# A five-engine instruction order set anew in a two-layer gated cross-attention kernel

## The reference

```python
# layer 0: cross-attention with rotary positions, then a ternary-weight MLP with squared ReLU and a low-rank term
q = rope(layernorm(x) @ Wq.T); k, v = split(ctx @ Wkv.T); k = rope(k)
x = x + tanh(g_xattn[0]) * (softmax(q k^T / 8) v) @ Wout.T
h = bitlinear(layernorm(x), w_fc) + gate * (layernorm(x) @ v.T @ fast_b.T @ u.T)
x = x + tanh(g_ffn[0]) * bitlinear(relu(h) ** 2, w_proj)
# layer 1: a linear mix with a row of the context, then an int8-activation, ternary-weight MLP
x = x + tanh(g_xattn[1]) * (layernorm(x) @ W1.T + mean_row(ctx) @ W2.T + b)
h = gelu(bitlinear(quant(rmsnorm(layernorm(x))), w1) + b1)
x = x + tanh(g_ffn[1]) * (bitlinear(quant(rmsnorm(h)), w2) + b2)
```

## Time and profile before

| | |
|---|---|
| three runs | 1253.99, 1259.77, 1259.27 us; median 1259.27 us |
| the profiled execution | 1254.16 us, of which its span 1252.1 us |
| busy, share of the span | PE 89%, DVE 78%, ACT 63%, POOL 46% |
| mean granted TensorE clock | 0.96 |
| chain of work that ended last | PE 30%, DVE 27%, ACT 20%, DMA 11%, issue 6%, POOL 4% |
| traffic | 140.28 MB, 112 GB/s mean; DMA share 0.91 in the first 135 us, 0.46 from 280 to 1144 us |

### The profile page before, as it was taken

One profiled execution on the slowest core, in us unless ns is written; L12 is line 12 of the kernel. 1 busy time (PEld: TensorE's weight loads), 2 busy tenths in 40 slices (PEclk: granted clock), 3 DMA queues, 4 the chain that ended last, 5 costly groups with the idle time before them and its releaser, 6 DMA issues.

```text
span 1252.1 us, 19955 instructions
## 1 busy us (share of the span) xinstructions
PE 1120.1 (89%) x7102; PEld 697.7 (56%) x7390; DVE 975.9 (78%) x2029; ACT 783.7 (63%) x1509; POOL 577.6 (46%) x564
## 2 busy tenths in 40 slices
PE   5737788989999999999899999999999999999973
PEld 3525546565665656474656565575657465565631
DVE  5998877678779787978877888878876867877672
ACT  2588765758393947576485858385767657585622
POOL 3121465445564644554545455555545443644330
PEclk9757799999999999999999999999999999999997
DMA  9959843463625354444536362637354353524122
GB/s 312 348 141 319 224 117 73 71 130 64 128 54 135 65 113 86 102 98 100 118 64 143 62 142 51 125 66 127 73 95 108 66 115 61 108 58 81 30 59 51
DMA packets 302242, 140.28 MB, mean 112 GB/s; under 512 B 258097, under 2 KB 276017, under 8 KB 300465
## 3 DMA queue, kind: packets, MB, share of 16 engines
q1 hardware_dynamic: 299840, 136.62, 48.7%
q10 hardware_dynamic: 2304, 2.40, 0.6%
HBM read 57.97 MB, written 9.18 MB: 54 GB/s over the span
## 4 chain that ended last, share of the span: by engine, by line
PE 30%; DVE 27%; ACT 20%; DMA 11%; issue 6%; POOL 4%; SPq 2%; POOLq 0%; ACTq 0%; DVEq 0%
PE ps L1734 8%; ACT e L937 5%; PE ps L1782 4%; PE ps L1685 4%; PE ps L1718 3%; ACT rl L975 3%; PE ps L1770 3%; DVE st L1334 3%; DMA pt<-qT 3%; PE ps L1750 3%; ACT hid L980 2%; DVE qT L1347 2%; ACT sq L986 2%; DVE amax L1041 2%; DMA hT<-q 2%
## 5 line engine op out<-in xcount | busy, mean ns | idle before, releaser
L1718 PE MATMUL ps<-xT,fcT 128*128 128x256 f16 x2048 | 261.4, 276 | 7.1 <-ACT rl L975 7.1
L719 POOL TENSOR_TENSOR rs<-ve,nhalf 128x1 f32<-128x1 f32 x160 | 105.3, 660 | 321.7 <-DVE ve L1339 226.4
L1734 PE MATMUL ps<-pjT,hid 128*128 128x512 fp8e4 x1024 | 232.6, 380 | 2.6 <-issue 1.3
L1718 PEld LDWEIGHTS ps<-xT,fcT 128*128 128x128 fp8e4 x2048 | 202.2, 99 | 42.2 <-ACT rl L975 10.2
L744 POOL TENSOR_TENSOR hid<-sq,hid 128x512 f16<-128x512 f32 x128 | 155.9, 1221 | 114.0 <-ACT sq L986 113.6
L1734 PEld LDWEIGHTS ps<-pjT,hid 128*128 128x128 f16 x1024 | 97.7, 98 | 98.9 <-issue 1.3
L1782 PE MATMUL ps<-w2T,hT 128*128 128x512 fp8e4 x512 | 119.9, 389 | 23.0 <-DMA hT<-q 22.8
L975 ACT ACTIVATE rl<-ps,rsf 128x256 f32<-128x256 f32 x256 | 106.5, 469 | 43.5 <-PE ps L1722 43.5
L1770 PE MATMUL ps<-w1T,q4T 128*128 128x512 fp8e4 x512 | 122.9, 383 | 5.6 <-DMA q4T<-x16b 4.5
L1007 ACT ACTIVATE q<-h 128x2048 f16<-128x2048 f32 x32 | 61.1, 1909 | 104.4 <-DVE h L1491 104.4
L937 ACT ACTIVATE e<-ps,nmb,sig 128x128 f32<-128x128 f32 x256 | 113.1, 458 | 4.7 <-DVE nmb L1377 4.5
(11 more groups left out here) (207 smaller groups left out, 1998.8 us busy)
## 6 DMA issues: line engine op xcount, KB each, us to landing
xb<-in_x SPq DMA_DIRECT2D x16, 512.0 KB, 4.2
qS<-qT SPq DMA_DIRECT2D x128, 64.0 KB, 2.1
out<-r SPq DMA_DIRECT2D x32, 256.0 KB, 2.4
xa<-in_x SPq DMA_DIRECT2D x15, 512.0 KB, 4.4
rope<-in_rope SPq DMA_DIRECT2D x16, 384.0 KB, 3.4
h<-in_w1T SPq DMA_DIRECT2D x6, 1024.0 KB, 6.2
h<-in_w2T SPq DMA_DIRECT2D x6, 1024.0 KB, 6.4
h<-in_wkvT SPq DMA_DIRECT2D x2, 1024.0 KB, 16.1
```

The lines of the kernel that those rows point to most:

```text
L1718: pe.matmul(dst, fcT[:, k, f * P:(f + 1) * P], xT2[:, xs, k, :], start=(xs == 0 and k == 0), stop=False)
L1734: mm = pe.matmul(ps[:, FFN0 + t, :], hid[:, xs, c, t * P:(t + 1) * P], pjT[:, c, :], start=(c == 0 and xs == 0), stop=(c == FC - 1 and xs ...
```

## The change

The numbers in ORDER and PREP are replaced. The tables take one line less, so every line behind them has a number lower by one. No operation, buffer, wait or semaphore is added or removed; each goes to another place in its own engine's list only. Of the 624 places of TensorE's operations 467 have another number, of VectorE's 784 608, of ScalarE's 496 342, of GpSimd's 544 344, of SyncE's 352 176; the median shift is 1 or 2 places and the largest 19.

```diff
...
-                pv=((24, 27), (52, 54), (85, 87), (120, 123), (164, 166), (201, 203), (241, 243), (279, 280),
...
+                pv=((23, 24), (52, 55), (87, 89), (120, 123), (161, 162), (203, 206), (240, 244), (276, 280),
...
-                pv=((40, 43), (78, 80), (107, 108), (138, 139), (170, 171), (200, 201), (231, 232), (262, 263),
...
```

296 lines of the change are left out of this document (148 added, 148 removed), and 132 rows, old and new, of tables (down, exp, h, hid).

## The result

The changed kernel takes 1247.99 us (median of 20 runs, 1242.29 to 1255.41), the kernel before 1253.3 us beside it (20 runs). The ratio is 0.9947, with a 95% interval of 0.993 to 0.9965: by the ratio 6.6 us faster (5.3 by the medians), where 16 were forecast (the sum of its four terms). The profiled execution of the changed kernel has a span of 1249.1 us against 1252.1.

What follows compares the result with a forecast made beforehand. VectorE, loads and serving order bound the front, TensorE (idle 32.8 of 864 us) the middle, one group's chain the end. 1254.16 - 3 - 2.5 - 4 - 6.5 = 1238.2, so a median of 1240 us; range 1225 to 1264.

Steps and rivals of the forecast that it cites:

- Front, -3 us: 0 to 135 us: neighbouring pv and an earlier wo could give 5.6 us; about half was taken.
- paid back before the last p_lo, so I count nothing for it: Front, VectorE: less work ahead of the first softmax, regained before the last p_lo; counted as nothing.
- set off against each other: Front: gain from group 0's second x2_hi ahead of an absolute sum, against row_scale behind a tern; net nothing.
- The bounds (+2 to -8): Front term's limits: +2 us if the conversions cost all of the gain, -8 us at best.
- 135 to 280 us and the middle, -2.5 and -4: -2.5 us: w2 of tile 1 covered by 26.9 us; -4 us: middle's small waits partly removed, from -12 to +29.
- the feared rival: Middle: pv waits longer for the transposed probabilities, 2.2 us of cover lost; 1259 us in 7 groups (0.13), 1273 in 13 (0.11).
- the prediction's zero: Group 14's last w1 to w2: cover 13.0 us instead of 17.3, 5.8 missing; counted at nothing, bound +4.
- The end, -6.5: From 1144 us on: 2.15 at group 15's first up, 3.0 from last down to w1, 1.3 from w1 to q5.
- The third term, 1.3 us: Last group: with the h split, q5 of tile 0 comes 13.3 us behind w1 instead of 14.6.
- the three terms: End: first up's wait covered (2.15 us), w1 sooner behind the last down (3.0), q5 sooner behind w1 (1.3).
- the slower side: Whole kernel slower: chance 0.12; its named case was 1273 us, probabilities 2.2 us late in all 13 groups (0.11).
- Meetings on shared buffers: Rival: one 0.93 us block in each of 14 groups on the chain to TensorE, +13, 1253 us; chance 0.12.

Runs made afterwards that it cites:

- front_only: Kernel before with the changed order only up to the low of group 1: 0.84% slower, 10.5 us.
- middle_and_end: Changed kernel with the old order up to the low of group 1: ratio 0.9872 to the kernel before, 16 us faster.
- middle_only: Kernel before with the changed order only from the low of group 1 to TensorE's place 604: 0.53% faster, 6.6 us.
- last_h_old: middle_and_end with VectorE's last fifteen places in the old order, the eight h in one row: 0.9927 against 0.9872, 6.9 us.
- end_only: Kernel before with the changed order only from group 15's first up on: no difference, ratio 0.9997.
- mix_later: Changed kernel with the mixing weights' product on TensorE moved behind the last scores of group 0: ratio 0.9940 to the kernel before.
- wq_first: Changed kernel with the query weights' load again first on SyncE's queue: ratio 0.9926 to the kernel before.
- norm1_late: Changed kernel with group 1's first norm again behind group 0's q rotation and the splitting of v: ratio 0.9971 to the kernel before.
- piece_behind: Changed kernel with a 1 MB piece's load moved from between group 0's two transpositions to behind the second: ratio 0.9935 to the kernel before.
- low_rank_early: Changed kernel with the low-rank scaling earlier on VectorE and its spread product earlier on TensorE: ratio 0.9993 to the kernel before.
- early_front_old: Changed kernel with the old order in the first part of the front, about the first 85 to 94 us: ratio 0.9900 to the kernel before.
- piece_between: middle_and_end with a 1 MB piece's load moved from ahead of the two transpositions to between them: ratio 0.9912 to the kernel before.
- early_old_piece: early_front_old with the 1 MB piece's load moved behind the two transpositions: ratio 0.9912 to the kernel before.
- sync_front_old: Changed kernel with SyncE's places 0 to 58 in the old order: ratio 1.014 to the kernel before, 24 us slower than the changed kernel.

## Why the prediction was wrong where it was

The sign was right, and the 1248.0 us lie in the range; 1240 was too low by 8. The miss in the change itself is larger, 16 us forecast and 6.6 measured: the kernel before came out at 1253.3 us, where the forecast had started from some 1256. Point by point:

- **Front, -3 us: the failed step.** The runs show +10.5 alone (front_only) and +9.4 with the rest in place (changed against middle_and_end). The prediction took one row of pairs, pv and pv and wo, counted what stood between them, and set what lies ahead of them and behind them to nothing: the work ahead of the softmax was "paid back before the last p_lo, so I count nothing for it", and the second x2_hi and row_scale were "set off against each other". In the profile the link that it did count was nearly right, 1.8 us won from pv to wo where it had 3. The two links at nothing cost 6.1 us ahead of pv and 4.7 from wo to low. In the second the prediction had misread the list: the second x2_hi still stands behind an absolute sum. The bounds (+2 to -8) left out the case that occurred. `mix`, the order of the loads and the load between two transpositions were in the list of the changed order and in no step of mine. With the old front the changed kernel measures 1238.1, and the sum without its front term is 1243.
- **135 to 280 us and the middle, -2.5 and -4: right in size, not in mechanism.** middle_only gives 6.6 us. The second w2 of group 0 has no wait now, as forecast. The waits for probabilities fell to 2.1 us although their cover is shorter, so the feared rival did not come. But w2's waits came up behind covers of 25 to 35 us (9.7 us in 8 waits), together with the wait for h, and TensorE's idle time from 280 to 1140 us did not fall (32.8 us both times). A cover counts TensorE's work alone; it does not say when VectorE comes to its part of the link. The shortest cover, 13.0 us, is that of group 14, and its wait is as before, 1.41 us for 1.47: there the prediction's zero was right. That the sum of this stretch fits is in part luck.
- **The end, -6.5: right in mechanism, too small in size.** There is no wait at the first up of group 15. It was worth more than its 2.15 us: behind it, from 1148.00 to 1152.63 us, the clock granted before was 0.63 of full speed, so for a part of this time TensorE ran at 1.2 GHz (shown below), and three up took 4.6 us where three take 2.9; now it is 1.00. From the last down (1198.08 - 1.38 = 1196.7) to w1 (1209.78) it is 13.1 us, forecast 12.4, before 15.4. The third term, 1.3 us, was mis-sized as well: q5 of tile 0 came 12.1 us behind w1 and not 13.3, and the square of tile 1 at 18.4 instead of 20.9, so 2.5 us. From that square on it takes 20.96 us to the end of the span, before 20.95. From place 605 to the end it is 7.9 us in the profile, and by the ratios of middle_only and middle_and_end 9.4. The prediction treated the three terms as separate. They are not: without the split of h, 6.9 us go (last_h_old), and without the changed middle the whole end brings nothing (end_only). The row of the kernel before, in the form of the earlier trace rows:

```profile
1148.00:1152.63 4.63, 4.63 (x28) 3.51 (x29) 4.27 (x12) 1.99 (x4) 3.65 (x4) 0.63 1.10 143
```

- **The sum's form.** The forecast added parts, and called the slower side a matter of the softmax link. The slower side did exist, and it was the front.
- **Meetings on shared buffers** as a reason for a loss: not seen. In the middle, hid_lo has the median and nearly the maximum of the earlier trace rows in the changed kernel too (below), TensorE waited for hid 0.5 us once, and the middle gained. No run changed such meetings alone.

```profile
L743 POOL TENSOR_TENSOR hid<-sq,hid x102: 1149/1157/2085, 282.8 to 1126.4; 128x512 f16<-128x512 f32 x102
```

**What stays open.** That the changed front costs about 10 us is shown twice (front_only, and middle_and_end against the changed kernel). With the old early part about half of it comes back, at the edge of the noise; the late part's 2.9 us are seen at the first low only. Which placements cause it is not shown. Five edits of one thing each in the changed front (mix_later, wq_first, norm1_late, piece_behind, low_rank_early), and two combinations of them, brought at most 0.2% against the changed kernel, which is within the intervals, and low_rank_early made it slower. One cause was shown up to the first low, the load between two transpositions; that it reaches the end of the kernel is not shown. What speaks for a spread loss is that a removed wait showed another behind it (mix_later, low_rank_early); that is an argument, not a proof.

## What to carry to other kernels

Count covers, and the places of the feeding operations on their own engines, for every operation in the stretch that is bound by many engines at once, also where the profile shows no long wait: a long wait that stands in parallel with others is worth nothing when removed, and a good order is lost by a change that looks harmless in one list. Where lists are to be mixed or compared, cut them at places with equal sets on every engine, and time the parts; a part can be worth nothing alone and 9 us behind another. On a queue that serves both, try a large load behind the second of two small transfers that the critical engine waits for, not between them.

## What the runs showed of the hardware

- A load of 1 MB issued between two transposing DMAs delayed the second: from its issue to the first use it took 7.6 us (changed kernel), 8.2 (early_front_old) and 6.9 (piece_between) with the load, and 5.1 (before), 5.4 (middle_and_end), 4.3 (piece_behind) and 3.4 (early_old_piece) without. The DMA share from 120 to 132 us was 1.06 in both middle_and_end and piece_between.
- TensorE's granted clock fell behind short waits: 0.63 over 4.6 us behind one of 2.15 us (before, 1148.00), 0.64 over 4.2 us behind one of 2.52 us (end_only, 1143.71). Behind one of 1.50 us (end_only, 1149.38) it was 1.00.
- The old order of one DMA queue's first 59 places, against the changed orders of the other engines, cost 24 us (sync_front_old): the largest effect of the study, from places alone.
- Profiles of kernels with identical order in a stretch differ there by up to 4 us (from the low of group 1 to that of group 4, with the changed middle: 201.6 us in wq_first, 205.6 in the changed kernel). The marks of the single profile of 1249.1 us gave the middle 3.2 us, the timed runs 6.6.
